# Local attention's last tiles: GpSimd normalises tiles 0 to 6 inside the stage, TensorE turns tiles 0 to 3

## The chip, the cores and the metric

The kernel runs on one NeuronCore of a Trainium2 chip. The metric is device time in microseconds (us). Three runs of the kernel before took 2576.57, 2580.86 and 2581.82 us; the median is 2580.86 us.

## What is computed

A residual stack of twelve layers works on x of 16 batches by 64 tokens by 256 features: 1024 tokens, held as eight tiles of 128 tokens. Each layer adds f(layernorm(x)) to x. The change sits at the seam between the second layer and the third:

```
x = x + _L0_attn_ref(_layernorm(x, axis=-1), w_qkv, ln_w, w_proj)      # local attention, 16 heads of 16
x = x + _L0_ffn_ref(_layernorm(x, axis=-1), gate_w, w1, w2, w3, ...)   # gate, top 2 of 8 experts, shared expert

def _layernorm(x, axis=-1, eps=1e-05):
    m = mean(x); v = var(x)
    return (x - m) / sqrt(v + eps)
```

The first thing that the third layer needs is layernorm(x) with its features on the partitions, since the gate's logits are layernorm(x) times a matrix of 256 by 8. So between the two layers each token tile is measured (mean and variance), normalised, and turned by TensorE.

## The kernel before, in words

The program is a row of stages. A stage has a list of instructions for each engine; an engine enters the next stage when all five have reported the end of the last (`Section.begin`, L94 to L97). So the time of a seam is: the last engine of the old stage, a barrier, and then whatever the new stage must do first. X (`x_tokens`) holds the tokens, xn (`xn_tokens`) the normalised ones, xnT (`xn_features`) the turned ones.

**The end of local attention** (second stage in `local_attention`, L4373 on). The batches are worked off in eight groups, group g being token tile g. The loop of each engine is a software pipeline over i = 0 to 11: TensorE does at step i the scores of group i (`scores`, L4424 and L4431, into `acc_s[i % 2]`), the transposes of the probabilities of group i-2 (`turn`, L4444), the products with the values of group i-3 (`mix`, L4459) and the output projection of group i-4 (`output`, L4472, all into the one bank `acc_y`). VectorE subtracts the maximum (L4539), normalises the probabilities (L4545, L4547 and L4549: a product of two SBUF operands), adds the projection to X (L4553), and measures that tile (`Statistics.tile`, L218 and L220). ScalarE takes the exponent and copies out of PSUM (L4494, L4500, L4506). GpSimd has nothing to do in this stage. At the end the statistics of all tiles are finished: ScalarE takes the square root of the eight variances (`Statistics.root`, L247, behind a table load), VectorE the reciprocal (L227) and the shift (L231). TensorE runs four idle products (`idle_products`, L511; eight records) into `spare`, the bank `acc_s[0]`.

**The gate's stage** (`gate_products`, L1478, through `normed_jobs`, L538). With `chip.normed_tiles` at 0, ScalarE normalises tiles 1, 4 and 6 (L681) and VectorE tiles 0, 2, 3, 5 and 7 (L645). TensorE runs one idle product, turns all eight tiles (`turn_tiles`, L574, sixteen transposes), and each half of the features is copied out of PSUM by ScalarE (L613) and VectorE (L657). Only then come the eight jobs, one for each tile: four products of 128 by 8 (L744), copied to `logits` by VectorE (L1484). Jobs 0 to 3 need the first half of the features, jobs 4 to 7 the second. They use four banks, so job 4 waits for the copy of job 0. SyncE loads six small tables meanwhile (L75).

**Where `chip.normed_tiles` is not 0** (call it first), `normed_jobs` takes tiles 0 to first-1 as normalised and the first half of xnT as there. VectorE measures tile 7 only, ScalarE takes its root, VectorE inverts it and normalises tiles first to 7. TensorE begins with jobs 0 to 3, then turns tiles 4 to 7 (`turn_rest`), ScalarE and VectorE copy one feature chunk each, and jobs 4 to 7 follow. In VectorE's order its feature copy stands ahead of all copies of logits.

**The class `Ahead`** (L253) is what another stage, the one-head attention before this one (L2523), uses already for six tiles: GpSimd adds epsilon to the variances (L268), raises them to the power -1/2 (L269) and normalises tile by tile (L272); TensorE turns tiles 0 to 3 (`turn`, L299); ScalarE copies the two chunks into xnT (`copy`, L306) and waits for the last normalised tile (`wait_normed`) before a square root of one column (L244) that leaves the table loaded. The stage behind it, the first of local attention, measures tile 7 with L4346 and L4348 and normalises tiles 6 and 7 with L4353.

**The stage behind the gate's** (`routed_experts`) begins with eight products of the shared expert (L1807, 128 by 512) on TensorE, beside VectorE's choice of experts (L1510 to L1527); the products that number the tokens (L1542) stand behind both.

Of the kernel before, what the change touches and what calls it, by code (L numbers as in the profile page):

```python
# [15 lines left out]
NT = T // P  # L16
# [5 lines left out]
HT = NT // 2  # L22
# [4134 lines left out]
def local_attention(chip, X, xn, xnT, ident, w, W, ahead):  # L4157
# [7 lines left out]
    GROUPS = NT  # L4165
# [17 lines left out]
    with ExitStack() as es:  # L4183
# [5 lines left out]
        with ExitStack() as inner:  # L4189
# [8 lines left out]
            with Stage(chip) as st:  # L4198
# [3 lines left out]
                block = st.block()  # L4202
# [174 lines left out]
        with Stage(chip) as st:  # L4377
# [4 lines left out]
            acc_s = [st.psum(P, 2, 8, S) for _ in range(2)]  # L4382
# [1 line left out]
            acc_m = late[0]  # L4384
            acc_y = st.psum(P, HALF)
            acc_v = [acc_t.rearrange("p i s -> p (i s)"), acc_y]
            spare = acc_s[0].rearrange("p y i s -> p (y i s)")
            (scored, max_ready, shifted, exp_done, summed, inverted, normed, turned, turned_copied, mixed, mixed_copied,
             y_filled, added, late_kept, v_filled, v_kept) = st.sems(16)
            statistics = Statistics(chip, st, X)  # L4390
            block = st.block()

            def blocks(t):
                return t.rearrange("p y c b n s -> p (y c b n) s")

            @block.sync
            def _(sync):
                st.clear_other_set(sync)
                for scratch in (chip.sent_rows, chip.done_rows):
                    sync.dma_start(scratch.rearrange("(n p) d -> p n d", p=P),  # L4400
                                   chip.zeros[:, :].unsqueeze(1).broadcast_to([P, TILES, D])
                                   ).then_inc(chip.rows_cleared, 16)
                slots = E * int(T / E * 1.25)
                sync.dma_start(chip.slots_sent[0:slots].rearrange("(n p) d -> p n d", p=P),
                               chip.zeros[:, :].unsqueeze(1).broadcast_to([P, slots // P, D])
                               ).then_inc(chip.slots_cleared, 16)
                for scratch in (chip.slots_done, chip.slots_early):
                    last = scratch.shape[0] - 1
                    sync.dma_start(scratch[last:last + 1], chip.zeros[0:1, :]).then_inc(chip.slots_cleared, 16)
                sync.wait_ge(v_filled, 2)  # L4410
                chip.load_far(sync, ahead)
                chip.wait_far(sync)

            @block.tensor
            def _(pe):
                def scores(g):
                    s = acc_s[g % 2]
                    if g == 0:
                        pe.wait_ge(chip.mask_ready, 2)
                    if g >= 2:  # L4420
                        pe.wait_ge(shifted, g - 1)
                    for y in range(2):
                        at = slice(y * S, y * S + S)
                        pe.matmul(s[:, y, :, :], twice[at, :], causal[at, :, :], start=True, stop=False)  # L4424
                    for c in range(DC):
                        for x in range(2):
                            b = 2 * g + x
                            for n in range(2):
                                for y in range(2):
                                    at = slice(y * S, y * S + S)  # L4430
                                    ins = pe.matmul(s[:, y, 4 * c + 2 * x + n, :], a[at, b, c, n, :, :],  # L4431
                                                    kT[at, c, b * S:b * S + S], start=False,
                                                    stop=(c == DC - 1 and x == 1 and n == 1))
                    ins.then_inc(scored, 1)

                def turn(g, x):
                    pe.wait_ge(normed, g + 1)
                    if g or x:
                        pe.wait_ge(turned_copied, 2 * g + x)
                    else:  # L4440
                        pe.wait_ge(v_kept, 1)
                    for y in range(2):
                        for c in range(DC):
                            ins = pe.transpose(acc_t[:, 2 * y + c, :],  # L4444
                                               probs[g % 3][:, y, c, x, :, :].rearrange("p n s -> p (n s)"), ident[:, :])
                    ins.then_inc(turned, 1)

                def mix(g):
                    pe.wait_ge(turned_copied, 2 * g + 2)
                    if g:  # L4450
                        pe.wait_ge(mixed_copied, g)
                    else:
                        pe.wait_ge(late_kept, 4 * DC)
                    for c in range(DC):
                        for x in range(2):
                            for y in range(2):
                                for k in range(2):
                                    t = 2 * y + k
                                    ins = pe.matmul(acc_m[t * 32:t * 32 + 32, (2 * c + x) * S:(2 * c + x + 1) * S],  # L4459
                                                    v[:, 2 * g + x, 4 * c + t, :],  # L4460
                                                    probsT[g % 2][:, x, 2 * y + c, k * S:k * S + S],
                                                    start=True, stop=True)
                    ins.then_inc(mixed, 1)

                def output(g):
                    pe.wait_ge(mixed_copied, g + 1)
                    if g:
                        pe.wait_ge(added, g)
                    else:
                        pe.wait_ge(v_kept, 2)  # L4470
                    for c in range(DC):
                        ins = pe.matmul(acc_y[:, 0:D], mT[g % 2][:, c, :], Wp[:, c, :], start=(c == 0), stop=(c == DC - 1))  # L4472
                    ins.then_inc(y_filled, 1)

                for i in range(GROUPS + 4):
                    if i < GROUPS:
                        scores(i)
                    if i < 2:
                        values(pe, acc_v[i], 2 + i).then_inc(v_filled, 1)
                    if 0 <= i - 2 < GROUPS:  # L4480
                        turn(i - 2, 0)
                    if 0 <= i - 3 < GROUPS:
                        mix(i - 3)
                    if 0 <= i - 2 < GROUPS:
                        turn(i - 2, 1)
                    if i >= 4:
                        output(i - 4)
                idle_products(chip, pe, spare, 4)

            @block.scalar  # L4490
            def _(act):
                def exponent(g):
                    act.wait_ge(shifted, g + 1)
                    act.activation(blocks(probs[g % 3]), blocks(probs[g % 3]), ACT.Exp).then_inc(exp_done, 1)  # L4494

                def keep(g, x):
                    act.wait_ge(turned, 2 * g + x + 1)
                    if g >= 2 and x == 0:
                        act.wait_ge(mixed, g - 1)
                    act.copy(probsT[g % 2][:, x, :, :], acc_t[:, :, :]).then_inc(turned_copied, 1)  # L4500

                def keep_mixed(g):
                    act.wait_ge(mixed, g + 1)
                    if g >= 2:
                        act.wait_ge(y_filled, g - 1)
                    act.copy(mT[g % 2][:, :, :], acc_m[:, 0:D].rearrange("p (c t) -> p c t", c=DC)).then_inc(mixed_copied, 1)  # L4506

                def keep_late(c):
                    for t in range(4):
                        act.activation(a[:, 8:16, c, t // 2, t % 2, :], late[c][:, :].rearrange("p (b s) -> p b s", s=S),  # L4510
                                       ACT.Copy, scale=side[:, c, t:t + 1]).then_inc(late_kept, 1)

                for i in range(GROUPS + 4):
                    if 0 <= i - 2 < GROUPS:
                        keep(i - 2, 0)
                    if 0 <= i - 3 < GROUPS:
                        keep_mixed(i - 3)
                    if 0 <= i - 2 < GROUPS:
                        keep(i - 2, 1)
                    if i < 2:  # L4520
                        act.wait_ge(v_filled, i + 1)
                        keep_values(act, acc_v[i], 2 + i).then_inc(v_kept, 1)
                    if i < GROUPS:
                        exponent(i)
                    if i < DC:
                        keep_late(i)
                statistics.root(act)

            @block.vector
# [251 lines left out]
```

## Time and profile before

| what | us |
|---|---|
| three runs | 2576.57, 2580.86, 2581.82 |
| the profiled execution's own time | 2570.98 |
| its span, from the first instruction to the last | 2569.2 |
| what lies around the span | 1.8 |
| TensorE busy in the span | 2459.1 (96%) |
| VectorE busy | 1460.7 (57%) |
| ScalarE busy | 997.6 (39%) |
| GpSimd busy | 702.0 (27%) |
| mean granted clock of TensorE | 0.987 of full |

Times in the trace are in us from the start of the span. The local attention's second stage runs from about 127.5 to 189.2, the gate's stage from 189.3 to 196.1. A row of the timeline gives start, duration, engine, line, operation, what it writes and reads, its shape and how many were merged; in brackets stands the engine's idle time ahead of it and what ended that. PE is TensorE's products, PEld its weight loads, DVE VectorE, ACT ScalarE, POOL GpSimd, SPq SyncE's queue of transfers. The profiled execution is 9.9 us shorter than the median of the three runs.

### The profile page before, as it was taken

What the parts mean: (1) busy time and instruction counts of PE and PEld (TensorE: products, weight loads), DVE (VectorE), ACT (ScalarE), POOL (GpSimd) and SP (SyncE); (2) the same over time, 40 slices, a digit from 0 to 9 for tenths busy, and PEclk for the clock granted to TensorE, in tenths of its full rate; (3) what the DMA queues carried; (4) which work ended last, traced back from release to release, by engine and by line L of the source; (5) the groups of instructions that cost most, each with busy time, mean ns of one, the idle gap of its engine ahead of it and who ended that gap; (6) DMA issues with size and microseconds to landing.
All of it is one profiled execution on the core that took longest, in us unless ns stands there. A gap on an engine that the chain in (4) does not pass through costs nothing. (4 is left out here: it accounts for less than half of the span.)

```text
span 2569.2 us, 46138 instructions
## 1 busy us (share of the span) xinstructions
PE 2459.1 (96%) x17970; PEld 1911.6 (74%) x17970; DVE 1460.7 (57%) x2413; ACT 997.6 (39%) x2153; POOL 702.0 (27%) x726
## 2 busy tenths in 40 slices
PE   7989998999999898999999999999999999989999
PEld 4666985666666657967888887895888888467778
DVE  5573227777777643035555556325555555689981
ACT  2352326666666322333222222223222222677741
POOL 2302011101010021013434432312344334058833
PEclk9989999999999999999999999999999999999999
DMA  9255873111110104952212212563121120032200
GB/s 322 98 171 185 313 247 75 34 34 51 34 34 18 56 33 159 332 166 68 73 62 63 73 39 108 191 221 113 55 73 63 62 72 16 28 111 83 83 17 17
DMA packets 93574, 260.38 MB, mean 101 GB/s; under 512 B 19267, under 2 KB 45543, under 8 KB 85831
## 3 DMA queue, kind: packets, MB, share of 16 engines
q1 hardware_dynamic: 81782, 240.34, 28.3%
q0 software_dynamic: 3840, 10.49, 1.3%
q10 hardware_dynamic: 7760, 6.89, 0.8%
q8 instruction: 135, 2.21, 0.4%
q14 instruction: 57, 0.46, 0.1%
HBM read 235.80 MB, written 21.86 MB: 100 GB/s over the span
## 5 line engine op out<-in xcount | busy, mean ns | idle before, releaser
L2907 POOL TENSOR_TENSOR buf<-buf 128x512 f32<-128x512 f32 x128 | 160.1, 1272 | 442.0 <-ACT buf L3057 441.8
L2973 PE MATMUL acc<-buf 128*128 128x256 f32 x1024 | 252.0, 379 | 0.0
L3091 DVE TENSOR_REDUCE buf<-acc 128x256 f32<-128x1024 f32 x124 | 151.8, 1225 | 158.1 <-PE acc L2939 158.1
L2939 PE MATMUL acc<-buf 128*128 128x256 f32 x992 | 229.3, 384 | 0.0
L3052 ACT COPY buf<-acc 128x256 f32<-128x256 f32 x62 | 23.1, 373 | 501.6 <-PE acc L2955 501.6
L2939 PEld LDWEIGHTS acc<-buf 128*128 128x128 f32 x992 | 183.4, 190 | 38.3 <-issue 15.9
L3557 ACT ACTIVATE buf<-acc,buf 128x512 f32<-128x512 f32 x256 | 172.6, 686 | 77.4 <-DVE buf L3589 77.4
L2973 PEld LDWEIGHTS acc<-buf 128*128 128x128 f32 x1024 | 184.7, 190 | 19.9
L3589 DVE TENSOR_REDUCE buf<-acc 128x1 f32<-128x512 f32 x256 | 159.0, 683 | 52.4 <-PE acc L3469 52.4
L3104 DVE TENSOR_TENSOR buf<-acc,buf 128x1024 f32<-128x1024 f32 x124 | 146.0, 1219 | 66.0 <-ACT buf L3052 66.0
L3057 ACT ACTIVATE buf<-buf 128x1024 f32<-128x1024 f32 x128 | 135.3, 1059 | 84.3 <-DVE buf L3104 80.0
L3603 DVE COPY buf<-acc 128x512 f32<-128x512 f32 x192 | 126.2, 685 | 53.9 <-PE acc L3481 53.6
L1831 PE MATMUL acc<-buf 128*128 128x128 f32 x1240 | 146.4, 276 | 4.0 <-DMA buf<-in_L_ffn_W 2.3
L1831 PEld LDWEIGHTS acc<-buf 128*128 128x128 f32 x1240 | 144.2, 192 | 7.7 <-issue 4.0
L4086 DVE TENSOR_TENSOR_SCAN buf<-buf,acc 128x1024 f32<-128x1024 f32 x64 | 142.7, 2269 | 8.7 <-PE acc L4003 5.8
L3481 PEld LDWEIGHTS acc<-identity,buf 128*128 128x128 f32 x1024 | 114.7, 141 | 42.9 <-issue 34.2
L3481 PE MATMUL acc<-identity,buf 128*128 128x128 f32 x1024 | 137.4, 277 | 4.7 <-DVE buf L3603 4.7
L2934 PE MATMUL acc<-buf 64*128 64x256 f32 x992 | 123.9, 389 | 2.7 <-DVEq L3131 2.7
L2980 PEld LDWEIGHTS acc<-buf 128*64 128x64 f32 x2048 | 110.6, 137 | 20.5 <-issue 20.5
L2980 PE MATMUL acc<-buf 128*64 128x128 f32 x2048 | 125.8, 276 | 0.0
L2934 PEld LDWEIGHTS acc<-buf 64*128 64x128 f32 x992 | 91.0, 186 | 22.6 <-issue 10.3
L1840 PE MATMUL acc<-buf 128*128 128x256 f32 x440 | 102.0, 384 | 2.3 <-DMA buf<-in_L_ffn_b 2.3
(549 smaller groups left out, 4781.2 us busy)
## 6 DMA issues: line engine op xcount, KB each, us to landing
buf<-in_L_ffn_W SPq DMA_DIRECT2D x52, 1024.0 KB, 6.9
buf<-in_ctx SPq DMA_DIRECT2D x48, 768.0 KB, 4.4
buf<-in_ctxT SPq DMA_DIRECT2D x62, 512.0 KB, 4.2
buf<-in_L_ffn_w SPq DMA_DIRECT2D x36, 640.0 KB, 5.7
buf<-state_rows SPq DMA_DIRECT2D x32, 512.0 KB, 4.1
buf<-in_L_ffn_w_and_w_tail SPq DMA_DIRECT2D x18, 768.0 KB, 4.4
buf<-in_ctxT SPq DMA_DIRECT2D x92, 128.0 KB, 4.5
buf<-in_ctxT SPq DMA_DIRECT2D x32, 256.0 KB, 5.5
```

What stands on the lines that cost most here:

```text
L1831: ins = pe.matmul(up(x, u, m), Wup[x][u][:, k, tile(m)], taken[x][:, k, :], start=(k == 0), stop=(k == DC - 1))
L2907: pool.tensor_tensor(quarters[:, 2 * n:2 * n + 2, :], t[:, 4 * n:4 * n + 2, :], t[:, 4 * n + 2:4 * n + 4, :], ALU.add).then_inc(adding, 1)
L2934: pe.matmul(acc_s[:, 4 * n + 2 * h + i, :], ct1[x][at, tile(k)], q1[at, b, 4 * y:4 * y + 4, :], start=(i == 0), stop=False)
L2939: ins = pe.matmul(acc_s[:, n, :], ct0[x][:, tile(key_tile(n))], q0[:, b, 4 * y:4 * y + 4, :], start=False, stop=(n % 2 == 1))
L2973: pe.matmul(acc_m[:, 0:ROWS], ctx[x][:, key_tile(n), 0:P], probsT[y][:, n, :], start=(n == 0), stop=(n == KT - 1))
L2980: ins = pe.matmul(acc_m[s * C1:s * C1 + C1, 2 * P:3 * P], ctx[x][:, key_tile(n), P:CC], probsT[y][:, n, tile(s)], start=(n == 0), stop=(n ...
L3091: dve.tensor_reduce(most_of[n][:, :], acc_s[:, 4 * n:4 * n + 4, :].rearrange("p k r -> p r k"), AX.X, ALU.max).then_inc(part_most, 1)
L3104: dve.tensor_tensor(probsT[p % 2][:, 4 * n:4 * n + 4, :], acc_s[:, 4 * n:4 * n + 4, :], most_all[:, :].unsqueeze(1).broadcast_to([P, 4, RO ...
L3481: ins = pe.transpose(acc_t[i % 2][:, k, :], probs[s % 2][:, i, tile(k)], ident[:, :])
L3557: act.activation(probs[s % 2][:, i, :], acc_s[i][:, :], ACT.Exp, bias=negmax[:, x, h, i:i + 1], accum_out=total[:, x, h, i:i + 1]).then_in ...
L3589: dve.tensor_reduce(negmax[:, s // 2 % 2, s % 2, i:i + 1], acc_s[i][:, :], AX.X, ALU.max, negate=True).then_inc(max_ready, 1)
L4086: dve.tensor_tensor_scan(state[n % STATES][:, :], decay[n % 2][:, :, :].rearrange("p b s -> p (b s)"), acc_d[n % 2][:, :], 0.0, ALU.mult, ...
```

## The change

At the end of local attention GpSimd gets a list: it normalises tiles 0 to 3 once tile 3 is measured, and tiles 4 to 6 once tile 6 is. TensorE turns tiles 0 to 3 at step 10 of its loop, ahead of `mix` of group 7, into `acc_s[0]`; the idle products go to `acc_s[1]` instead. ScalarE, after its loop, copies the two chunks of features to the first half of xnT, waits until seven tiles are normalised, and takes the root of one column. VectorE no longer measures tile 7 and no longer forms the reciprocal and the shift. `chip.normed_tiles` is 7, so the gate's stage takes its other way. The whole diff:

```diff
@@ local_attention, second stage @@
-            spare = acc_s[0].rearrange("p y i s -> p (y i s)")
+            spare = acc_s[1].rearrange("p y i s -> p (y i s)")
...
-            statistics = Statistics(chip, st, X)
+            statistics = Statistics(chip, st, X, ahead=True)
+            next_norm = Ahead(chip, st, statistics, xn, NT - 1)
+            first_features = acc_s[0].rearrange("p y i s -> p y (i s)")
...
+            @block.gpsimd
+            def _(pool):
+                next_norm.normalise(pool, range(0, HT))
+                next_norm.normalise(pool, range(HT, next_norm.tiles))
...
                     if i < 2:
                         values(pe, acc_v[i], 2 + i).then_inc(v_filled, 1)
+                    if i == GROUPS + 2:
+                        pe.wait_ge(shifted, GROUPS - 1)
+                        next_norm.turn(pe, lambda c, j: first_features[:, c, tile(j)])
                     if 0 <= i - 2 < GROUPS:
                         turn(i - 2, 0)
...
                     if i < DC:
                         keep_late(i)
+                next_norm.copy(act, lambda c: first_features[:, c, :], xnT)
+                next_norm.wait_normed(act)
                 statistics.root(act)
```

Not in the diff, but called by it:

```python
    def normalise(self, pool, tiles):                       # Ahead, L264
        n, s, at = self.chip.norm, self.statistics, slice(tiles.start, tiles.stop)
        pool.wait_ge(s.measured, 2 * tiles.stop)
        c = Chain(pool, self.rooted, self.links)
        c.link(pool.tensor_scalar(n.spread[:, at], n.mv[:, at, 1], EPS, None, ALU.add))
        c.link(pool.tensor_tensor(n.rstd[:, at], n.spread[:, at], n.minus_half[:, at], ALU.pow))
        self.links += c.n
        for j in tiles:
            pool.tensor_scalar(self.keep[:, j, :], s.src[:, j, :], n.mv[:, j, 0:1], n.rstd[:, j:j + 1],
                               ALU.subtract, ALU.mult).then_inc(self.normed, 1)

    def turn(self, pe, acc):                                # L295
        for j in range(HT):
            pe.wait_ge(self.normed, j + 1)
            for c in range(DC):
                ins = pe.transpose(acc(c, j), self.keep[:, j, tile(c)], self.chip.ident[:, :])
        ins.then_inc(self.turned, 1)
```

## Rows read from the trace of the kernel before

**Rows 1.** The head of the profile's page
```profile
span 2569.2 us, 46138 instructions
```

**Rows 2.** Busy time by stretch (us busy, count): the gate's stage and the stretch behind it
```profile
189.30:196.10 6.80, 6.49 (x50) 5.97 (x50) 4.24 (x15) 2.75 (x5) 0.00 (x0) 0.92 0.12 25
196.10:202.50 6.40, 6.30 (x9) 2.73 (x10) 5.02 (x22) 1.88 (x2) 0.00 (x0) 0.56 0.00 0
```

**Rows 3.** Timeline, the end of local attention
```profile
177.30 0.18 DVE L220 BATCH_NORM_AGGREGATE buf<-buf 128x2 f32<-128x6 f32 x1
...
178.91 1.23 DVE L4549 TENSOR_TENSOR buf<-buf 128x1024 f32<-128x1024 f32 x1
...
183.71 0.65 PE L4459 MATMUL acc<-buf 128*32 128x64 f32 x32
...
184.38 1.10 PE L4472 MATMUL acc<-buf 128*128 128x256 f32 x4
...
184.82 1.28 ACT L247 ACT_TABLE_LOAD   x1
...
186.44 0.18 DVE L220 BATCH_NORM_AGGREGATE buf<-buf 128x2 f32<-128x6 f32 x1
...
187.03 1.89 PE L511 MATMUL acc<-zeros,identity 128*128 128x256 f32 x8
...
188.36 0.30 ACT L247 ACTIVATE buf<-buf 128x8 f32<-128x8 f32 x1 [2.26 <-DVE buf L220]
```

**Rows 4.** Timeline, the gate's stage and the first instruction of the next
```profile
189.37 1.71 DVE L645 TENSOR_SCALAR xn_tokens<-x_tokens,buf 128x256 f32<-128x256 f32 x5 [0.27 <-POOLq L127]
...
189.84 1.97 PE L574 MATMUL acc<-identity,xn_tokens 128*128 128x128 f32 x16
...
190.99 0.68 DVE L657 COPY xn_features<-acc 128x512 f32<-128x512 f32 x1
...
191.72 4.08 PE L744 MATMUL acc<-first_weights,xn_features 128*128 128x8 f32 x32
...
195.84 0.17 DVE L1484 COPY buf<-acc 128x8 f32<-128x8 f32 x1 [0.62 <-PE acc L744]
196.16 1.28 ACT L1883 ACT_TABLE_LOAD   x1 [3.73 <-DVEq L111]
```

**Rows 5.** Timeline, GpSimd in the one-head stage
```profile
78.96 1.05 POOL L269 TENSOR_TENSOR buf<-buf 128x4 f32<-128x4 f32 x1
...
91.58 0.24 POOL L268 TENSOR_SCALAR buf<-buf 128x2 f32<-128x2 f32 x1 [6.59 <-DVE buf L220]
91.90 0.73 POOL L269 TENSOR_TENSOR buf<-buf 128x2 f32<-128x2 f32 x1
92.73 2.44 POOL L272 TENSOR_SCALAR xn_tokens<-x_tokens,buf 128x256 f32<-128x256 f32 x2
```

**Rows 6.** Timeline, the start of local attention: tile 7 measured, tiles 6 and 7 normalised
```profile
103.03 0.43 DVE L4346 BATCH_NORM_STATS2 buf<-x_tokens 128x6 f32<-128x256 f32 x1 [1.44 <-DVE x_tokens L2714]
...
104.24 2.78 DVE L4353 TENSOR_SCALAR xn_tokens<-x_tokens,buf 128x256 f32<-128x256 f32 x2
```

**Rows 7.** Timeline, VectorE's L3094 (two SBUF operands) beside GpSimd, at two places
```profile
1178.47 1.27 POOL L2910 TENSOR_TENSOR buf<-buf 128x512 f32<-128x512 f32 x1
...
1178.67 1.35 DVE L3094 TENSOR_TENSOR buf<-buf 128x256 f32<-128x256 f32 x1
...
2166.49 1.24 POOL L272 TENSOR_SCALAR xn_tokens<-x_tokens,buf 128x256 f32<-128x256 f32 x1
...
2167.46 0.42 DVE L3094 TENSOR_TENSOR buf<-buf 128x256 f32<-128x256 f32 x1
```

**Rows 8.** Busy time by stretch, with columns as in rows 2: TensorE idle, and after it
```profile
382.40:387.90 5.50, 0.00 (x0) 0.00 (x0) 4.04 (x13) 0.98 (x3) 4.12 (x5) 0.84 0.34 103
387.90:392.40 4.50, 2.20 (x8) 1.29 (x8) 3.58 (x10) 2.91 (x6) 0.95 (x1) 0.50 0.19 58
...
1607.70:1612.00 4.30, 0.04 (x1) 0.00 (x0) 3.48 (x16) 1.28 (x1) 0.00 (x0) 0.54 0.02 4
```

The columns of rows 2 and 8 are: the stretch and its length, then busy us and instructions of TensorE's products, its weight loads, VectorE, ScalarE and GpSimd, then TensorE's granted clock as a share of full speed, the DMA engines' busy share and GB/s.

## The prediction

> **What bounds the kernel now.** I read the page's head first: the profiled execution took 2570.98 us, 1.8 us of it outside its span [rows 1]. A measurement of this kernel can tell about 0.2%, 5.2 us, from no change. One seam of twelve stages is touched, so the averages of busy time say nothing; the timeline of the seam does. In it the reader is to see what ends last in each stage.
>
> The end of local attention is a chain of single steps: mix of group 7 at 183.71, output of group 6 at 184.38, its addition and measurement, which end at 186.62 (186.44 + 0.18) [rows 3], then the same for group 7, the root of eight columns at 188.36 on ScalarE (0.30) and two small operations on VectorE. The table load for that root, at 184.82, is long over: it stands ahead of the wait that the root itself has [rows 3]. The gate's stage starts at about 189.3: normalising at 189.37 on VectorE, sixteen transposes from 189.84 (1.97 us), a feature copy (0.68), 32 products from 191.72 (4.08), the last logits at 195.84; the stage behind starts at 196.16 [rows 4]. So the stage takes 6.86 us, and TensorE is busy for 6.49 us of it [rows 2]. Behind it TensorE runs at half its clock for most of 6.4 us (granted clock 0.56) [rows 2].
>
> **The change, part by part.** Times are in the clock of the trace of before.
>
> *GpSimd's second group becomes the end of the stage.* It may start when tile 6 is measured, 186.62. From the same class in the one-head stage [rows 5]: epsilon's addition to the power 0.32 (91.58 to 91.90); the power takes 0.73 for two columns and 1.05 for four, so about 0.89 for three; 0.10 to the first tile; a tile is 1.22 (2.44 for two), so 3.66 for three. With 0.1 for the answer to the semaphore that is 5.07, and ends at 191.69. ScalarE waits for it, and then does its root of one column, at most 0.30 [rows 3]. From the last instruction to the next stage it was 0.15 (196.01 to 196.16) [rows 4]. The stage would end at 192.15 to 192.2 instead of 189.3: **+2.9**. What VectorE saves (measuring tile 7, reciprocal, shift) lies in its shadow and is worth nothing. The table load could stand behind the wait for GpSimd, which would cost 1.28 more, or nothing; I take nothing, as at 184.82 it ran ahead of its root's wait [rows 3].
>
> *GpSimd's first group delays TensorE.* Tile 3 is measured at 177.48 (177.30 + 0.18). GpSimd then needs 0.1 + 0.32 + 1.05 + 0.10 to the first tile, 179.05, and 4.88 for four: 183.93. TensorE comes to step 10 at 183.71. Tiles 0 to 2 are turned as they come; for tile 3 it waits, and its two transposes and the way to the next weights take about 0.35. So mix starts at 184.3 instead of 183.71, and output, addition, measurement, GpSimd's second group and everything queued behind on TensorE (output of group 7, the idle products) move by **0.6**. That is the lower value. But VectorE's L4549, a product of two SBUF operands, starts at 178.91 for 1.23 us [rows 3], just ahead of GpSimd's first tile. What such a pair can do is seen elsewhere [rows 7]: L3094 took 1.35 us when GpSimd's L2910 had started 0.2 ahead of it, and 0.42 when L272 was in its last 0.27. One stood until the other had finished. If L4549 has the port, the first tile ends 1.1 later, and the delay is **1.7**. I take 1.7, as the nearest in kind (two operands against a read) shows a full stop [rows 7]. The upper value is the reverse order: GpSimd first, L4549 1.35 later, TensorE with it, and then all eight transposes (0.98) on the path: 2.3.
>
> The Trainium skill's page "SBUF — State Buffer", section "Who interferes with whom", states that a Vector instruction with two SBUF inputs contends with a GpSimd instruction that reads SBUF, and that whoever is second waits for the whole instruction. By that rule the delay is 1.7 or 2.3, without it 0.6; the 0.42 beside L272's end [rows 7] doesn't decide, since only its tail overlapped.
>
> *ScalarE* gets two copies of features, and they run beside GpSimd's second group: nothing. If that group were gone, they would still lie beside output of group 7. TensorE's new wait for the shift of group 6 is long fulfilled. No transfer and no instruction of SyncE is moved.
>
> *The gate's stage gets shorter.* Removed: one idle product, eight transposes of sixteen, two of four feature copies, eight normalisations on two engines. Added: tile 7's measuring, root, reciprocal and normalisation, where in local attention the normalisation starts 1.21 behind the measuring (103.03 to 104.24) [rows 6]; the first of the two tiles there took long because GpSimd's memset ran beside it, and here GpSimd is idle. With about 0.4 (five in 1.71 [rows 4], less their overlap) it is ready at 1.6, while TensorE needs its first 16 products (half of 4.08, 2.0) before it turns anything: hidden. Then 0.98 for eight transposes, 0.7 for the copy, 0.25 until job 0's logits are out and TensorE answers, 2.0 for the other jobs, 0.4 for the last copy and the barrier: 6.3 against 6.86, **-0.5**. The products are first now, but the second half still ends the stage.
>
> *TensorE's clock.* The idle products end at 188.92 (187.03 + 1.89) [rows 3], plus the delay, and the stage's end moves with the same delay: so TensorE stands idle for about 3.3 us, where it stood 0.4. Then come products of 8 columns. Where it was idle for 5.5 us before [rows 8], the granted clock was 0.84 in that stretch and 0.50 in the 4.5 us behind; and in 4.3 us without work behind the gate's products of another layer it was 0.54 [rows 8]. At half clock the PE-paced parts of the new gate's stage (2.0 + 1.0 + 2.0) take twice as long. Bounds: nothing, and +5.0. I take **+3.0**: the clock falls after the first jobs, and the three us left take six.
>
> **The sum:** 2.9 + 1.7 - 0.5 + 3.0 = **+7.1 us**. Against the profiled execution's own time: 2570.98 + 7.1 = 2578.1. The median of the three runs is 9.9 above that execution; with the same difference the median would be 2580.86 + 7.1 = **2588.0**. The lowest sum is 2.9 + 0.6 - 0.5 = +3.0, the highest 2.9 + 2.3 - 0.5 + 5.0 = +9.7.
>
> **The rivals.**
> 1. *The clock stays up in the gate's stage.* Place: 194.0 to 200. For it: 3.3 us of idle time is less than the 5.5 and 4.3 of the other places [rows 8], and dense idle products stand ahead of it. Against it: products of 8 columns alone were followed by 0.56 [rows 2]. Sum +3.0 to +4.1, 2583.9 to 2585.0: within 0.2%. Chance 0.22.
> 2. *Not slower: the clock gives back behind the gate.* The eight products of L1807 run at 0.56 for 6.4 us now [rows 2]. If the low stretch falls into the idle gap instead, and the clock is up when they start, they take 3.2 less; the gate keeps its +4.1: +0.9, 2581.8. It decides if TensorE's clock is full within a microsecond of that stage's start; and VectorE's choice, busy for 5.02 of the 6.4 beside them [rows 2], must not become the bound, which speaks against it. Chance 0.07.
> 3. *GpSimd takes the port first.* L4549 and all behind it wait: 2.9 + 2.3 - 0.5 + 3.0 = +7.7, 2588.6. The two starts are 0.14 apart, so it can be. Chance 0.07.
> 4. *The seam gains,* because GpSimd's tiles or the wait for them are shorter than in the one-head stage [rows 5], or the change does not do what it says (the long tail isn't waited for). Even then only the 0.5 of the gate and a clock effect of up to 3.2 are to be had, so -3.7, 2577.2; over 0.2% only with the spread of the runs. Chance 0.06.
>
> **How the numbers follow.** The forecast has 0.58, with rival 3 that is 0.65 for slower by over 0.2%; rivals 1 and 2 give 0.29 for within; rival 4 gives 0.06 for faster. The three runs spread from 4.3 below their median to 1.0 above. The range goes from 2579.5 (rival 2 less half of that spread) to 2592.5 (the highest sum, 2590.6, and 1.9 for the spread).
>
> **What would show it.** Right: L272 in the stage with seven tiles, the last ending some 5 us behind the measurement of tile 6; ScalarE's L244 as the stage's last instruction; the first tile of L272 longer than 1.24 (about 2.3); mix of group 7 behind L299; the gate's stage from 194 on, beginning with L744, and its stretch at a clock well below 0.92. Wrong: the stage ending before 191; a gate's stage under 6 us; the stretch of L1807 at a clock near 1; or VectorE's L4549 longer than 1.23, which is rival 3.

## Result, and the profile of the changed kernel

| | median us | runs | lowest to highest | profiled execution |
|---|---|---|---|---|
| before | 2581.18 | 8 | 2575.62 to 2588.11 | 2570.98 |
| changed | 2589.14 | 8 | 2583.80 to 2600.99 | 2583.80 |

The ratio is 1.0035, with a 95% interval of 1.0021 to 1.0049. Times 2581.18 that is 9.0 us slower, between 5.4 and 12.6; the medians are 8.0 apart. The forecast was +7.1 and 2588.0.

The page's head of the changed kernel, which answers to [rows 1]:

```profile
span 2582.0 us, 46139 instructions
...
PE 2457.9 (95%) x17968; PEld 1911.6 (74%) x17968; DVE 1457.8 (56%) x2407; ACT 996.9 (39%) x2152; POOL 714.3 (28%) x737
```

TensorE is busy for 2457.9 us, where it was 2459.1. The share of its time says nothing about a loss of 9 us, as the prediction held; only the seam does. Here is the timeline of the changed kernel's seam, which answers to [rows 3, 4]. Every line number of local attention behind the diff is 7 to 12 higher: L4459 is now L4466, L4472 is L4479, L4549 is L4561; the root is L244 where it was L247.

```profile
182.42 0.18 DVE L220 BATCH_NORM_AGGREGATE buf<-buf 128x2 f32<-128x6 f32 x1
...
183.01 1.04 POOL L269 TENSOR_TENSOR buf<-buf 128x4 f32<-128x4 f32 x1
...
184.03 1.23 DVE L4561 TENSOR_TENSOR buf<-buf 128x1024 f32<-128x1024 f32 x1
184.16 5.83 POOL L272 TENSOR_SCALAR xn_tokens<-x_tokens,buf 128x256 f32<-128x256 f32 x4
...
188.07 0.60 PE L299 MATMUL acc<-identity,xn_tokens 128*128 128x128 f32 x4
...
188.83 0.44 PE L299 MATMUL acc<-identity,xn_tokens 128*128 128x128 f32 x2 [0.16 <-POOL xn_tokens L272]
...
190.03 0.44 PE L299 MATMUL acc<-identity,xn_tokens 128*128 128x128 f32 x2 [0.77 <-POOL xn_tokens L272]
...
190.40 0.65 PE L4466 MATMUL acc<-buf 128*32 128x64 f32 x32
...
192.48 1.28 ACT L244 ACT_TABLE_LOAD   x1
...
193.07 0.18 DVE L220 BATCH_NORM_AGGREGATE buf<-buf 128x2 f32<-128x6 f32 x1
...
193.66 1.89 PE L511 MATMUL acc<-zeros,identity 128*128 128x256 f32 x8
193.67 0.87 POOL L269 TENSOR_TENSOR buf<-buf 128x3 f32<-128x3 f32 x1
...
194.65 3.65 POOL L272 TENSOR_SCALAR xn_tokens<-x_tokens,buf 128x256 f32<-128x256 f32 x3
198.33 0.29 ACT L244 ACTIVATE buf<-buf 128x1 f32<-128x1 f32 x1 [4.57 <-POOL xn_tokens L272]
...
198.79 1.92 PE L744 MATMUL acc<-first_weights,xn_features 128*128 128x8 f32 x16 [3.24 <-POOLq L127]
...
200.57 1.85 PE L574 MATMUL acc<-identity,xn_tokens 128*128 128x128 f32 x8
...
202.46 0.69 DVE L653 COPY xn_features<-acc 128x512 f32<-128x512 f32 x1 [2.05 <-PE acc L574]
...
203.37 3.55 PE L744 MATMUL acc<-first_weights,xn_features 128*128 128x8 f32 x16 [0.95 <-DVE buf L1484]
...
206.96 0.17 DVE L1484 COPY buf<-acc 128x8 f32<-128x8 f32 x1 [0.69 <-PE acc L744]
...
207.31 5.47 PE L1807 MATMUL acc<-xn_features,first_weights 128*128 128x512 f32 x8 [0.40 <-DVEq L111]
```

Read it from the top. Tile 3 is measured at 182.60 (182.42 + 0.18). GpSimd's four tiles take 5.83, not four times 1.22, and TensorE's last turn waits 0.77 for the fourth of them, so that mix of group 7 starts at 190.40. Tile 6 is measured at 193.25; GpSimd's three tiles end at 198.30, ScalarE has waited 4.57 us for them, and its root of 0.29 is the stage's last instruction. TensorE has stood idle for 3.24 us when the gate begins at 198.79, with its products. Its first sixteen products take 1.92. Everything behind them takes nearly twice as long: the eight transposes 1.85, and the second sixteen products 3.55.

The busy time by stretch shows why, with the columns of [rows 2]: the wait of the stage's end, the gate's stage, and the stretch behind it, of the changed kernel.

```profile
193.30:198.76 5.46, 2.25 (x11) 1.64 (x10) 0.42 (x1) 0.76 (x2) 4.77 (x5) 1.00 0.00 0
198.76:207.28 8.52, 7.18 (x40) 6.74 (x40) 2.83 (x13) 0.89 (x3) 0.00 (x0) 0.61 0.08 18
207.28:212.62 5.34, 5.31 (x9) 2.31 (x10) 4.57 (x21) 1.88 (x2) 0.00 (x0) 0.66 0.01 3
```

The granted clock in the gate's stage is 0.61, where it was 0.92 [rows 2], and the stretch behind it has 0.66, where it had 0.56: TensorE fell to the lower of its levels (1.2 for 2.4 GHz) early in the gate and stayed there, and it is not back when L1807 begins.

To put numbers on the parts I cut the seam at five points that every version has: tile 3 measured (end of its L220), tile 6 measured, the start of the gate's stage and its end (TensorE's jump into the next code, 0.1 us ahead of its first product there), and the first product of L1542 behind the choice. The last column says how long after the gate's start the clock fell, read from stretches of 0.1 us.

| trace | tile 3 to 6 | tile 6 to the gate | gate's stage | behind it | seam | clock falls at |
|---|---|---|---|---|---|---|
| before | 9.14 | 2.58 | 6.89 | 6.39 | 25.00 | 5.8 |
| before, second trace | 8.47 | 2.58 | 6.56 | 5.31 | 22.91 | 7.3 |
| before, third trace | 9.88 | 2.58 | 6.60 | 4.99 | 24.06 | 6.1 |
| changed | 10.65 | 5.43 | 8.52 | 5.41 | 30.01 | 2.0 |
| changed, second trace | 10.64 | 5.42 | 9.66 | 5.92 | 31.63 | 0.8 |

The mean of two traces is 30.8 and that of three is 24.0: +6.8. Of the difference of the first two executions (12.8 us), 5.0 lies in the seam, 5.1 ahead of it (tile 3 was measured at 182.60 instead of 177.48) and 2.7 behind it.

The part ahead of the seam is in code that no part of the change touches, but it comes back in every changed trace. In the one-head attention TensorE waits for a transfer of `in_ctxT`, in the trace of before and in that of the change:

```profile
44.17 1.94 PE L2587 MATMUL acc<-buf 128*64 128x512 f32 x8 [1.73 <-DMA buf<-in_ctxT]
```

```profile
44.24 3.33 PE L2587 MATMUL acc<-buf 128*64 128x512 f32 x8 [3.21 <-DMA buf<-in_ctxT]
```

VectorE's first L2714 behind these waits starts at 48.58 to 49.73 in the three traces of before, and at 50.48 to 54.62 in the eleven of the changed kernel and its versions: all of them are later, by 3.0 on the mean. Why is not shown, and no run was made for it. At tile 3 the means are still 2.9 apart (179.6 and 182.5), but there single traces overlap.

### The profile page after: what moved, and what is told of

Read it like the earlier page. It is cut to its first block and busy times, and to the rows that moved or that the text cites. A ratio compares the mean times of both kernels' runs of the same rounds, so it can differ in the third digit from the quotient of the medians.

```text
span 2582.0 us, 46139 instructions
## 1 busy us (share of the span) xinstructions
PE 2457.9 (95%) x17968; PEld 1911.6 (74%) x17968; DVE 1457.8 (56%) x2407; ACT 996.9 (39%) x2152; POOL 714.3 (28%) x737
## 3 DMA queue, kind: packets, MB, share of 16 engines
q10 hardware_dynamic: 7760, 6.89, 0.8%
```

## Experiments

Each is one edit of the changed kernel. Each group of experiments has its own runs of before beside it, with medians of 2582.75 (31 runs), 2584.16 (16) and 2580.73 (17).

**Is the wait for GpSimd's second group the end of the stage, and what is it worth?** Theory: the stage ends when its last L272 has ended, and starting tiles 4 and 5 earlier, or leaving tile 6 out, takes exactly that out of the time. Rival: the clock alone costs the time. First, each tile as soon as it is measured:

```diff
-                next_norm.normalise(pool, range(HT, next_norm.tiles))
+                for j in range(HT, next_norm.tiles):
+                    next_norm.normalise(pool, range(j, j + 1))
```

> GpSimd takes tiles 4, 5 and 6 one at a time, each with its own wait, epsilon and power. I read the seam as the time from the end of tile 3's measurement (L220) to L1542's first product: 25.0 us before, 30.0 with the change. Path theory (GpSimd's chain ends the stage, each of its microseconds counts): tiles 4 and 5 start when the first group is done (189.99 in the changed kernel's trace), each takes 2.2 (0.32 + 0.57 + 0.10 + 1.22), so the last ends at about 196.7 and not 198.3: the seam 1.6 us shorter, 28.4; the time 1.6 us under the change. Clock theory (the loss is TensorE's idle time and the low clock, the tail itself costs only through it): TensorE's idle time falls from 3.2 to 1.6, the gate's stretch is at full clock, and the seam is 3 or more shorter. If tile 6's end is not what ends the stage: no difference.

Timeline of this version, the stage's end:

```profile
193.54 0.18 DVE L220 BATCH_NORM_AGGREGATE buf<-buf 128x2 f32<-128x6 f32 x1
...
195.79 1.23 POOL L272 TENSOR_SCALAR xn_tokens<-x_tokens,buf 128x256 f32<-128x256 f32 x1
197.06 0.29 ACT L244 ACTIVATE buf<-buf 128x1 f32<-128x1 f32 x1 [2.83 <-POOL xn_tokens L272]
...
197.52 1.92 PE L744 MATMUL acc<-first_weights,xn_features 128*128 128x8 f32 x16 [1.50 <-POOLq L127]
```

From tile 6 measured to the gate is 3.69 instead of 5.43, and the seam is 28.32 instead of 30.01: the tail lost 1.74 (the gate's stage and what is behind it moved by -0.8 and +0.8 against each other). The median is 2591.71 (12 runs), the ratio to before 1.0029 (1.0016 to 1.0041). ScalarE still waits 2.83 us, for tile 6 alone. Then six tiles only, so that tile 6 is left to the gate's stage, as tile 7 is:

```diff
-            next_norm = Ahead(chip, st, statistics, xn, NT - 1)
+            next_norm = Ahead(chip, st, statistics, xn, 6)
```

> GpSimd normalises six tiles and not seven; VectorE takes tiles 6 and 7 in the gate's stage (its second tile is 0.4 us, hidden behind TensorE's first products). Path theory: the second group waits for tile 5 and ends about 193.6 in the changed kernel's clock, so the idle products (195.55) end the stage and the next starts at 195.7 and not 198.8: the tail from tile 6's measurement to the next stage 2.4 and not 5.5, the time 3.1 us under the change, and less again by what the clock gives. Clock theory: TensorE's idle time ahead of the gate is 0.2, as before the change, so the gate's stretch has before's clock and the seam is 25.0 or less. Both say the change is repaired but for the delay of 1.6 us on TensorE; they differ in whether the gate's stage takes 6.3 (path, clock no worse than before) or under it. If the tail is no cost: no difference.

Timeline of the version with six tiles:

```profile
190.98 2.44 POOL L272 TENSOR_SCALAR xn_tokens<-x_tokens,buf 128x256 f32<-128x256 f32 x2
...
192.96 0.18 DVE L220 BATCH_NORM_AGGREGATE buf<-buf 128x2 f32<-128x6 f32 x1
...
193.55 1.89 PE L511 MATMUL acc<-zeros,identity 128*128 128x256 f32 x8
193.66 0.29 ACT L244 ACTIVATE buf<-buf 128x1 f32<-128x1 f32 x1
...
195.67 1.92 PE L744 MATMUL acc<-first_weights,xn_features 128*128 128x8 f32 x16 [0.23 <-POOLq L127]
```

Now L272 ends at 193.42, near tile 6's measurement at 193.14. ScalarE's root no longer waits, and the idle products are the stage's last work. Tile 6 to the gate is 2.43, below before's 2.58. The gate's stage took 6.59, and the seam 25.92. The median is 2587.77, the ratio 1.0017 (1.0001 to 1.0032). The tail is gone, and the gate's stage is 1.9 shorter in this trace than in the change's; the delay stands (10.65).

**Does VectorE's product hold GpSimd's first tile?** Theory: L4561, with two SBUF operands, starts 0.13 ahead of L272, and L272 stands until it has ended. Rival: the first tile of a group is long by itself (GpSimd has stood idle for 56 us before it). The edit starts the group behind VectorE's product of the last group, and changes nothing but that moment:

```diff
             def _(pool):
+                pool.wait_ge(normed, GROUPS)
                 next_norm.normalise(pool, range(0, HT))
```

> GpSimd's first group waits until VectorE's last product of two SBUF operands (L4561 for group 7) is done; the work is the same. Port theory (the first tile of L272, 2.2 us with the change, stood still while L4561 held the port): all seven tiles take 1.21 to 1.24, the first group ends where it did or up to 0.4 later (its epsilon and power come behind the product too: 1.4 later at most), L4561 stays 1.22. Rival (a first instruction of its kind costs 1 us more on GpSimd, wherever it stands): the first tile again 2.2.

Timeline of that version:

```profile
181.13 1.23 DVE L4562 TENSOR_TENSOR buf<-buf 128x1024 f32<-128x1024 f32 x1
...
183.90 4.84 POOL L272 TENSOR_SCALAR xn_tokens<-x_tokens,buf 128x256 f32<-128x256 f32 x4
...
188.79 0.44 PE L299 MATMUL acc<-identity,xn_tokens 128*128 128x128 f32 x2 [0.76 <-POOL xn_tokens L272]
```

With no such product beside it all four tiles take 4.84, 1.22 the first and 1.21 each of the others; in the changed kernel it was 5.83, of which the first took 2.20. VectorE's product is 1.23 in both. GpSimd was idle for as long ahead of it (54.96 us), so a long first use is out, and it is the pair: GpSimd came second by 0.13 and stood for 0.98 of the 1.10 us that the product still had. The Trainium skill's rule, page "SBUF — State Buffer", section "Who interferes with whom" (whoever is second waits for the whole instruction), agrees with these rows in this order; for the other order see below. The later start costs more than the stop did: tile 3 to 6 is 12.31. In this trace the clock was low from the gate's start (gate's stage 10.25), and the one execution took 2596.81.

**How much of the delay is the turn on TensorE's path?** Tiles 0 to 2 as soon as tile 2 is measured, tile 3 by itself:

```diff
-                next_norm.normalise(pool, range(0, HT))
+                next_norm.normalise(pool, range(0, HT - 1))
+                next_norm.normalise(pool, range(HT - 1, HT))
```

> GpSimd takes tiles 0 to 2 as soon as tile 2 is measured, tile 3 on its own. Path theory: tile 3 is normalised about 2.3 us (3.4 if L4561 has the port) behind its measurement and not 7.4, TensorE no longer waits at step 10, only its eight transposes (about 1.0) remain of the delay of 1.6: the time 0.6 us under the change, the tail of 5.5 and the gate's 8.5 as they are. Rival (the waits of GpSimd and VectorE for the port decide): GpSimd's tiles 0 to 2 now meet the probabilities' product (L4561) of group 6, two SBUF operands; if GpSimd is first there, L4561 takes up to 2.4 instead of 1.23, and the whole is up to 1 us slower than the change.

Tile 3 to 6 took 9.70 instead of 10.65, and the rest of the seam changed little (5.43, 8.82, 5.10 for 5.43, 8.52, 5.41). The total did not follow: 2594.19 (8 runs), ratio 1.0045 (1.0027 to 1.0062), not below the change's. One us is too small against the spread of these runs, so the seam's trace is the evidence here, and the total is a miss. Then both groups split (those lines are left out here), and the turn one step later, behind mix of group 7 and output of group 6, where TensorE waits ahead of its last output:

```diff
...
-                    if i == GROUPS + 2:
+                    if i == GROUPS + 3:
                         pe.wait_ge(shifted, GROUPS - 1)
```

> Seven tiles, both groups split, TensorE's turning one step later. Path theory: tile 3 to tile 6 measured in 8.2 to 8.6; GpSimd's last tile 2.3 behind tile 6's measurement, and then ScalarE's root, so the tail is 2.9 at best (3.2 if tile 5's is still under way) against 5.4 with the change and 2.6 before; TensorE's idle products end later than that or just then. Seam 25 to 26. Rival (GpSimd is the bound with seven tiles in any order, since it has 2.2 us for each tile and they are measured every 1.7 at the end): tail over 4.

Tile 3 to 6 fell to 8.52, what before takes at full clock (8.47), and tile 6 to the gate to 3.16. The seam was 25.73, the gate's stage 7.75 of it; the one execution took 2584.56. The same with six tiles:

> Three repairs at once: six tiles and not seven, tiles 0 to 2 ahead of tile 3 and tiles 4 and 5 one at a time, and TensorE's turning one step later, ahead of the output of group 7, where it stood idle for 0.6 us anyway. Path theory: from tile 3's measurement to tile 6's 8.2 us at full clock (10.65 with the change), the tail 2.4 to 2.9, the gate's stage 6.3 to 6.6, to L1542 another 6.3: seam 24.0 or less, as short as before the change or up to 1 us shorter; the time within 1 us of before (0.04%), which five rounds can't tell. Clock theory (light products first bring the clock down early whatever the tail is): the gate's stage 7.5 or more and the time 2 us or more over before.

Timeline of the version with six tiles, both splits and the later turn:

```profile
178.43 4.67 POOL L272 TENSOR_SCALAR xn_tokens<-x_tokens,buf 128x256 f32<-128x256 f32 x3
...
180.85 1.25 DVE L4563 TENSOR_TENSOR buf<-buf 128x1024 f32<-128x1024 f32 x1
...
184.19 1.24 POOL L272 TENSOR_SCALAR xn_tokens<-x_tokens,buf 128x256 f32<-128x256 f32 x1
...
184.53 1.28 DVE L4563 TENSOR_TENSOR buf<-buf 128x1024 f32<-128x1024 f32 x1
...
190.33 1.04 PE L299 MATMUL acc<-identity,xn_tokens 128*128 128x128 f32 x8
...
192.07 1.89 PE L511 MATMUL acc<-zeros,identity 128*128 128x256 f32 x8
...
194.24 1.92 PE L744 MATMUL acc<-first_weights,xn_features 128*128 128x8 f32 x16 [0.28 <-POOLq L127]
...
198.03 3.51 PE L744 MATMUL acc<-first_weights,xn_features 128*128 128x8 f32 x16 [0.94 <-DVE buf L1484]
```

The first four rows are read in the last section. The eight turns are one row of 1.04 without a wait, and TensorE is idle for 0.28 ahead of the gate. Tile 3 to 6 is 8.53, tile 6 to the gate 2.50: both terms of the change are gone. The seam is 23.82, inside before's 22.9 to 25.0, and the time is before's too: 2587.49 (12 runs) against 2584.16, ratio 1.0009 (0.9996 to 1.0021). So taking out these two terms takes the seam back to before's; the total is before's within an interval that still allows 5.4 us. What is left of it is the gate: 7.70 against before's 6.56 to 6.89, with the second sixteen products at 3.51.

**Why does the clock fall early in the gate?** Theory A: TensorE's idle gap ahead of the gate brings it down. Theory B: the gate's own products of 8 columns, first now, do. The gap was filled with idle products, ten and then eleven in place of four:

```diff
-                idle_products(chip, pe, spare, 4)
+                idle_products(chip, pe, spare, 10)
```

> Ten idle products and not four at the end of local attention, so TensorE is busy until the stage ends; nothing else moves. Path theory: tail 5.5 and delay 1.6 stay, the gate's stage goes from 8.5 to at most 6.9 if the clock stays up to its last jobs: 1.6 to 2.2 us under the change, still 5 or more over before. Clock theory: the loss is the clock, so nearly all 8 us come back and the kernel is within 1 us of before. No clock effect: the gate's stage stays at 8.5.

The gap shrank from 3.24 to 0.63, and against the change's first trace nothing changed: seam 29.99 for 30.01, gate's stage 8.50 for 8.52, the clock down at 2.03 for 2.01. (The change's second trace has 31.63, 9.66 and 0.8.) The median is 2590.64, the ratio 1.0024 (1.0009 to 1.0039).

> Eleven idle products and not four: TensorE is busy up to the barrier. With ten, the low clock began 2.03 us into the gate's stage, with four 2.01. Idle theory (the 0.5 us left without work brought it down): it now begins 5 us in, the gate's stage takes under 7. Light-product theory (the products of 8 columns bring it down, whatever stood ahead of them): again about 2 us in, the stage 8.5.

Timeline with eleven:

```profile
193.40 4.91 PE L511 MATMUL acc<-zeros,identity 128*128 128x256 f32 x22
...
198.59 1.92 PE L744 MATMUL acc<-first_weights,xn_features 128*128 128x8 f32 x16 [0.28 <-POOLq L127]
...
202.38 3.55 PE L744 MATMUL acc<-first_weights,xn_features 128*128 128x8 f32 x16 [0.95 <-DVE buf L1484]
```

TensorE works until 198.31 and begins again at 198.59. The clock fell at 3.9, the gate's stage took 7.74, and the second sixteen products again 3.55; the seam was 28.94, and the one execution took 2585.53. The gap is not the whole cause, since with and without it the clock falls before the gate's stage ends. But all traces together don't clear it either:

| gap ahead of the gate, us | clock falls at | gate's stage |
|---|---|---|
| 3.2 (changed twice, split first group, start behind the product) | 2.0, 0.8, 1.7, 0.0 | 8.52, 9.66, 8.82, 10.25 |
| 1.5 (tiles 4 to 6 one by one) | 2.9 | 7.74 |
| 0.9 (seven tiles, later turn) | 3.1 | 7.75 |
| 0.6 (ten idle products) | 2.0 | 8.50 |
| 0.2 to 0.3 (six tiles; six tiles with later turn; eleven idle products) | 5.2, 4.0, 3.9 | 6.59, 7.70, 7.74 |

The stage takes 9.3 on the mean with the long gap and 7.7 with the shorter ones. So a long gap goes with an earlier fall, though not in every trace: with the ten idle products it came at 2.0, and in the version with the filler below at 2.6 with a gap of 0.28. These versions differ in other things too. With one trace each, what share the gap has, and what sets the moment, can't be told. Last, two filler products in the gate itself, in TensorE's wait for the feature copy, on top of the version with both terms gone:

```diff
...
                     turn_rest(pe)
+                    if first == 6 and jobs[0][2][1] == E:
+                        idle_products(chip, pe, turned[0][0], 2)
```

> The repaired kernel of before (six tiles, split groups, later turning), and in the gate's stage two idle products on TensorE behind the transposes of tiles 4 to 7, where it stands 0.9 us waiting for the copied features. Light-product theory (the products of 8 columns bring the clock down): the low stretch begins later, the gate's stage takes 6.5 to 7.0 and not 7.7; the time 0 to 1 us under the repaired kernel. If two idle products are too few: 7.7 as before, or 7.8 to 8.1 where they hold up job 4 at the low clock (two of them take 0.9 at full and 1.9 us at half).

Timeline of the gate's stage with the filler (L746 is L744):

```profile
190.11 1.92 PE L746 MATMUL acc<-first_weights,xn_features 128*128 128x8 f32 x16 [0.28 <-POOLq L127]
...
191.89 1.27 PE L574 MATMUL acc<-identity,xn_tokens 128*128 128x128 f32 x8
...
192.95 1.92 PE L511 MATMUL acc<-zeros,identity 128*128 128x256 f32 x4
...
194.65 3.42 PE L746 MATMUL acc<-first_weights,xn_features 128*128 128x8 f32 x16
```

The four instructions of filler took 1.92, not 0.95, since the clock had fallen ahead of them, and the products behind them had to wait for their end. The gate's stage took 8.36 where it was 7.70 without them: a miss. (The clock also fell sooner in this trace, at 2.6 for 4.0, so the difference isn't all the filler's.) The total is before's, 2580.26 (12 runs) against 2580.73, ratio 1.0003 (0.9987 to 1.0019). No version beat before.

**How far do two traces of one kernel differ?** Before twice more, and the change once:

> The kernel before, unchanged, for a second trace with the low-clock stretches at other places. In the first trace one of them lay in the stretch from tile 3's to tile 6's measurement (9.14 us), and the change's trace had none there (10.65). If the delay by GpSimd's first group is the 1.5 of that comparison, before takes 9.1 again at full clock; if the low clock hid part of it, before takes 8.2 at full clock and the delay is 2.5. The seam (tile 3 measured to L1542) is then 23.5 to 25 and not fixed at 25.0.

> The kernel before a third time, for the same question: the tail from tile 6's measurement 2.6 in every trace, the gate's stage between 6.5 and 7.5 by where the clock falls, tile 3 to tile 6 8.2 without a low stretch and up to 9.2 with one.

> The changed kernel, unchanged, for a second trace. Path theory: tile 3 to tile 6 10.65 and the tail 5.4 whatever the clock does, as GpSimd sets both; only the gate's stage (8.5 in the first trace) and the stretch to L1542 vary, the gate's stage between 6.3 and 11. If the 10.65 was TensorE's own work at some clock, it moves with the clock.

They gave 2577.60, 2586.17 and 2599.36 us, and the rows of their seams in the table above. The second trace of before, timeline and stretches (local attention's end, the gate's stage, the stretch behind it):

```profile
180.05 0.18 DVE L220 BATCH_NORM_AGGREGATE buf<-buf 128x2 f32<-128x6 f32 x1
...
185.79 0.65 PE L4459 MATMUL acc<-buf 128*32 128x64 f32 x32
```

```profile
191.30:197.90 6.60, 6.16 (x50) 5.66 (x50) 4.24 (x15) 2.76 (x5) 0.00 (x0) 1.00 0.12 26
197.90:203.20 5.30, 5.26 (x10) 2.27 (x10) 4.52 (x21) 1.88 (x2) 0.00 (x0) 0.68 0.00 0
```

Here the clock was full from tile 3 to the end of the gate, and fell 0.7 us later. Mix of group 7 came 5.56 behind tile 3's measurement; in the trace that I predicted from it was 6.23, with TensorE at its lower clock from 177.9 to 181.3. In the second trace of the change TensorE was at its lower clock from 183.5 to 186.8, and tile 3 to 6 still took 10.64: there GpSimd sets the time, and not TensorE's clock.

## Why the prediction was right, and where it was not

The mechanism came as forecast: the wait for GpSimd's tiles, the delay by the first group, and a gate's stage at the lower clock. The sizes of the delay and of the clock agreed partly by luck.

**The tail, +2.9.** Measured 5.43 and 5.42 for 2.58: +2.85. Its parts came as worked out from the one-head stage [rows 5]: the power of three columns 0.87 (0.89 estimated), three tiles 3.65 (3.66), the root of one column 0.29. The table load at 192.48 ran ahead of the root's wait, so its 1.28 was hidden. Removing the wait (six tiles) brought 2.43: shown by experiment.

**The delay, +1.7.** Mix of group 7 was forecast 7.9 behind the measurement of tile 3 (6.23 + 1.7) and came at 7.80. The port's full stop, the value chosen from [rows 7] against the lower 0.6, is shown by the 4.84 for 5.83; the reverse order (rival 3) did not occur, as L4561 is 1.23. Its price was wrong as well: where GpSimd's tile stood first in later versions, VectorE's product took 1.28 and not 1.35 more (last section). By those rows the reverse order would have added next to nothing, and 2.3 was too high a bound; it wasn't tried on the changed kernel itself. But the base was too slow: before's trace had a low-clock stretch in it, and at full clock before needs 5.56. So against a like clock the change costs 2.2, and against the mean of three traces (9.16) 1.5. The term was right for the trace it was worked out from, and is not a property of the kernel. That 1.5 comes near it is luck, since the base of that mean has low-clock stretches too.

**The gate's stage, -0.5.** At full clock the eight transposes take 1.07 (the version with eleven idle products, and four others), not the 0.98 that the prediction took. Take from the changed trace what the low clock added to its two rows: 8.52 less 0.78 (transposes, 1.85 for 1.07) and less 1.63 (3.55 for 1.92) is 6.1. In its second trace 9.66, less 1.04 (2.96 for 1.92 in the first products), 0.88 and 1.63, is 6.1 too. Before's, at full clock throughout, is 6.56. So the forecast's -0.5 holds.

**The clock, +3.0.** The same subtraction gives +2.4 in the one trace and +3.55 in the other. Their mean is the forecast, but that is luck in part: 3.0 was chosen between 0 and 5, and two versions with the same gap, by the same subtraction, have 2.7 and 4.1. The prediction's wording, "the clock falls after the first jobs", held in the first trace (2.0 us in); in the second it fell among them (0.8). Its reasons named the idle gap ahead of the gate beside the products of 8 columns. Filling the gap to 0.63 us changed nothing against the first trace, while over all traces a short gap goes with a later fall; so a part for the gap is neither shown nor excluded, and what decides the moment is open. Rival 1 (clock up in the gate) is out for the change: no version with the products first kept it up to the stage's end, though the one with six tiles kept it for 5.2 of 6.59 us. Rival 2 (giving back behind the gate) is out as well: the stretch of L1807 has 0.66, and "behind it" is 5.41 and 5.92, where before has 4.99 to 6.39. Rival 4 fell with the tail.

**The sum.** 2.85 + 1.5 + 2.4 for the gate with its clock (9.09 for 6.68, forecast -0.5 + 3.0 = 2.5) + 0.1 behind it = +6.8, against a forecast of 7.1 and 9.0 (5.4 to 12.6) by the ratio. What lies between 6.8 and 9.0 is within the interval. But the traces show one place for it that the prediction did not have: the first 50 us of the program, later in every changed trace, by 3.0 on the mean. Whether that belongs to the change is open; the version with the filler has it too (50.48) and took no longer than before in all.

## What to carry to other kernels

Work given to a slower engine is hidden only up to the time its last input leaves: here GpSimd needs 5 us behind a measurement that lay 2.6 ahead of the stage's end, so give it only the tiles whose chain fits (six, each as measured) and put what consumes them into a wait that TensorE has anyway (here ahead of its last output), not ahead of a step that others wait for. Look then at what comes first in the stage behind: here light products came first, the dense work after them ran at the lower clock, and that cost as much as the tail. Even with both terms of GpSimd's gone no version was faster than before: the 0.5 that the new gate's stage saves at full clock goes in what the lower clock costs it; the shortest of these stages took 6.59, where before has 6.56 to 6.89. And take the base of each step from more than one trace, since one low-clock stretch in it hid 0.7 us.

## What was not expected

- **The pair does not block alike in both orders.** Take the first four rows of the version with the later turn. Three tiles take 4.67 from 178.43, so the first two end at about 180.87; VectorE's L4563 starts at 180.85, and the third tile takes some 2.26 where 1.22 is its own time: GpSimd stood, and VectorE took 1.25. But at 184.19 GpSimd is first by 0.34, they overlap for 0.90, and neither stands: 1.24 and 1.28. The same in three more of the versions (1.24 beside 1.28 or 1.29). The Trainium skill's page "SBUF — State Buffer", section "Who interferes with whom", says that the second blocks fully, whichever it is; in this order the rows don't agree, and they decide. A pair with two SBUF operands on either side did block in this order [rows 7]. VectorE's product with one operand in PSUM (L4551 of the changed kernel) overlapped a tile by 0.97 to 0.98 in four versions, and neither stood (1.22 to 1.23 each), as that page of the Trainium skill has it. Whether the exception is a matter of the operation's kind, or how early GpSimd has read its operand, wasn't tried.
- **The runs of one kernel differ with TensorE's clock.** Over 31 runs of before the mean granted clock went from 0.980 to 0.987 and the time from 2593 down to 2576. That is 17 us for 0.007 of clock, more than the whole change, so a single execution can't weigh a term of 1 or 3 us in its total; the seam can.
- **Idle products bought little where they were tried:** six more ahead of the gate left the seam at 29.99 for the first trace's 30.01, seven more had 28.94 (one trace), and with two inside it the stage took 8.36 for 7.70.
